# Two gated attention layers: ScalarE's order of key copies, exponential and token normalisation, and where the scores wait

## The chip, the cores and the metric

The kernel runs on one NeuronCore of a Trainium2 chip. Its engines work side by side and are ordered by semaphores alone: TensorE (PE, matmuls), VectorE (DVE), ScalarE (ACT), GpSimd (POOL) and SyncE (SP, which issues DMAs). The metric is the device time of one execution in microseconds. The kernel before took 2021.08 us, the median of 3 runs.

## The reference, cut to what matters

```python
x = x + tanh(g_xattn[0]) * L0_xattn(layernorm(x), ctx_768, ...)   # 8 heads of 64
x = x + tanh(g_ffn[0])   * L0_ffn(layernorm(x), ...)              # 16 experts, chosen by a Sinkhorn
x = x + tanh(g_xattn[1]) * L1_xattn(layernorm(x), ctx_768, ...)   # 16 heads of 64
x = x + tanh(g_ffn[1])   * L1_ffn(layernorm(x), ...)              # 2 of 8 experts for each sequence

# an attention:
q, k, v = x @ Wq, context @ Wk, context @ Wv
out = softmax(q @ k.T * 64 ** -0.5) @ v
out = out @ Wo + bo
```

x is 128 sequences of 64 tokens with 128 features, the context 128 x 64 x 96, all float32.

## The kernel before, in words

Tokens are worked on in 64 tiles of 128 (two sequences). `attention` builds both attention layers. The products of weights are folded beforehand: `AT` takes the context to keys that are multiplied directly with the tokens, `Bw` takes it to values that already hold the output projection. A step j handles one unit, a tile with 8 heads: the first attention has 64 units (G = 1), the second 128 (G = 2, two units for each tile; a unit "opens" its tile when it is the first of the two). Float16 operands are split in a high and a low part, which makes three products of each.

Each engine runs its own `body(j)` for every step, and in one body it handles several units at once: a is unit j, a1 is unit j-1, and so on. A semaphore wait at one point of an engine's order holds everything behind it. What belongs to step j, in the order in which each engine takes it:

- PE: in the second attention the transpose of the tile's normalised tokens (`psX`, L626, after ACT's `ln`), then the b half of the values of unit j-3 (L599), the keys of unit j in two halves of four heads, 24 matmuls each (L610, `psU`), the output product of unit j-4 (L654, `psY`, which waits for the transposed probabilities `PT` and for both value halves), the a half of the values of unit j-2 (L599), and the scores of unit j (L679, `psS`), two matmul pairs for heads 0 to 3, then two for heads 4 to 7. Ahead of the scores it waits for the tokens (`xt`), for both key copies (`uc0`, `uc1`) and for DVE's subtraction of the step before (`sub`). In the first attention the token transpose stands after the b values and is for the next unit, and a transpose of the context (L666) stands before the scores.
- ACT: normalised tokens (L713), high part of the values (L697, half a), transposed tokens `xTa` (L706), high part (L697, half b), the exponential of unit j-1 (L722, after `sub`), the two copies of the keys from PSUM (L728, 128 x 512 each, after `U0` and `U1` of PE), and the high part of the probabilities of unit j-2 (L733, after POOL's `mul`).
- DVE: low part of the values, half b (L802), sum of the exponentials of unit j-1 (L811) and its reciprocal (L813), residual (L817), maximum of the scores of unit j (L821), subtraction (L824), statistics for the next layer norm (L177), low part of the values, half a (L802). In the first attention it also works the layer norm of later tiles into some of its steps.
- POOL: bo added to x (L762, after `ln`), multiplication by the reciprocal (L776, unit j-1), low part of the probabilities (L781, unit j-2).
- SP: loads of context and keys, and the DMA transpose `PT<-Ph` of unit j-2 (L549).

In the second attention the keys of 40 tiles' second units (AHEAD = 40) were made earlier and lie in HBM. So in steps 0 to 79 the odd steps load their keys (L563, `a.loaded`) and only the even ones compute them; in steps 80 to 127 every step computes them. `phases` runs these two stretches, each with some steps in straight line and the rest in a hardware loop over 8 steps. There is one `psS`, and one `psU` bank for each half of the heads.

Of the kernel before, what the change touches and what calls it, by code (L numbers as in the profile page):

```python
# [18 lines left out]
ACT = mybir.ActivationFunctionType  # L19
# [10 lines left out]
AHEAD = 40  # L30
# [45 lines left out]
def wait(eng, sem, step, per=1, add=0):  # L76

    if isinstance(sem, Counter):
        sem, add = sem.handle, add + sem.start
    if step.reg is None and step.times(per, per + add) <= 0:  # L80
        return
    eng.wait_ge(sem, step.times(per, per + add))


def pipeline(eng, body, first, last, lo, hi, unroll):

    a = min(-(-lo // unroll) * unroll, last)
    n = max(0, (hi - a) // unroll)
    b = a + n * unroll
    for j in range(first, a):  # L90
        body(Step(None, 0, j))
    if n:
        with eng.Fori(0, n) as i:
            for u in range(unroll):
                body(Step(i, unroll, a + u))
    for j in range(b, last):
        body(Step(None, 0, j))
# [7 lines left out]
def _build(nc, whole, I, out):  # L105
# [66 lines left out]
    def column_of(t, tensor):  # L172
        return tensor[:, bass.ds(t.value, 1)]
# [166 lines left out]
    def attention(tag, G, Wq, Wk, Wv, Wo, bo, gate, ew=None, rw=None):  # L340

        first = ew is not None
        U = NT * G
        INNER = 512 * G
        s = Sems(tag)
        with ExitStack() as c:
# [154 lines left out]

                return (t - slot).div(n)

            def phases(eng, body, last, lo, hi):

                if first:
                    pipeline(eng, body, 0, last, lo, hi, 4)
                else:
                    pipeline(eng, body, 0, 2 * AHEAD, lo, 2 * AHEAD, RING * G)
                    pipeline(eng, body, 2 * AHEAD, last, 2 * AHEAD + 4, hi, RING * G)  # L510

            with nc.Block() as block:
# [76 lines left out]
                def _(e):  # L589
                    def body(j):  # L590
# [77 lines left out]
                        if a.on:  # L668
                            if a.opens:
                                wait(e, s["xt"], a.t)  # L670
                            if a.loaded:
                                wait(e, s[f"ul{a.tp}"], ring_of(a.t, 2, a.tp), 16)
                            else:
                                wait(e, s["uc0"], a.key())
                                wait(e, s["uc1"], a.key())
                            wait(e, s["sub"], a.j - 1)
                            for h in (0, 4):
                                for b in range(2):
                                    last = e.matmul(psS[half(b), h:h + 4, :], xT[:, a.tp, half(b)],  # L679
                                                    u[:, a.slot, h:h + 4, half(b)], start=True, stop=True)  # L680
                            last.then_inc(s["S"], 1)
# [7 lines left out]
                @block.scalar  # L689
                def _(e):  # L690
                    def body(j):
                        a, a1, a2, a3 = (Unit(j, k) for k in range(4))

                        def value_hi(a, b, name):
                            wait(e, s["V" + name], a.j)
                            wait(e, s["PV"], a.j - 2)
                            e.activation(vB[:, a.par, 0, b].rearrange("p k d -> p (k d)"), a.values(b),  # L697
                                         ACT.Copy).then_inc(s["vh" + name], 1)

                        nx = Unit(j, -1) if first else a  # L700

                        def tokens():
                            if nx.opens:
                                wait(e, s["X"], nx.t)
                                wait(e, s["S"], nx.j - G - 1)
                                e.activation(xT[:, nx.tp, :], psX, ACT.Copy).then_inc(s["xt"], 1)  # L706

                        if first and nx.on:
                            wait(e, s["C"], nx.t - 2)
                            e.activation(cc[:, nx.tp, 0, 0:DC], tile_of(nx.t, ctx32), ACT.Copy).then_inc(s["chi"], 1)  # L710
                        if nx.opens:
                            wait(e, s["X"], nx.t - 2)
                            e.activation(xn[:, nx.tp, :], tile_of(nx.t, x), ACT.Identity, bias=column_of(nx.t, nmr),  # L713
                                         scale=column_of(nx.t, rstd)).then_inc(s["ln"], 1)
                        if a3.on:
                            value_hi(a3, 0, "a")
                        tokens()
                        if a3.on:
                            value_hi(a3, 1, "b")
                        if a1.on:  # L720
                            wait(e, s["sub"], a1.j)
                            e.activation(E[:, a1.four], E[:, a1.four], ACT.Exp, bias=zero_col[:], scale=DH ** -0.5)\  # L722
                             .then_inc(s["exp"], 1)
                        if a.on and not a.loaded:
                            wait(e, s["S"], a.j - 2)
                            for b in range(2):
                                wait(e, s[f"U{b}"], a.key())
                                e.activation(u[:, a.slot, 4 * b:4 * b + 4].rearrange("p h l -> p (h l)"),  # L728
                                             psU[:, b, :], ACT.Copy).then_inc(s[f"uc{b}"], 1)
                        if a2.on:  # L730
                            wait(e, s["mul"], a2.j)
                            wait(e, s[f"pt{a2.par}"], ring_of(a2.j, 2, a2.par) - 1, 16)
                            e.activation(Ph[:, a2.par, 0].rearrange("p k t -> p (k t)"),  # L733
                                         E[:, a2.four].rearrange("p h l -> p (h l)"), ACT.Copy)\
                             .then_inc(s["phi"], 1)
                        if first and nx.on:
                            wait(e, s["C"], nx.t)
                            wait(e, s["Vb"], nx.j - RING)
                            wait(e, s[f"stored{nx.ring}"], ring(nx.t, nx.ring) - 1, 16)
                            e.activation(cT[:, nx.ring], psC[0:DC], ACT.Copy).then_inc(s["ct"], 1)  # L740
                    if first:
                        parts = (0, 8, 16, 32, 48, U)
                        for part, (lo, hi) in enumerate(zip(parts, parts[1:])):
                            e.wait_ge(s["nmr"], part + 1)
                            e.wait_ge(s[f"c{lo}"], 64 if lo >= 32 else 16)
                            pipeline(e, body, lo - 1, hi - 1 + 4 * (hi == U), max(lo - 1, 8), hi - 1, 4)
                    else:
                        e.wait_ge(s["nmr"], 1)
                        phases(e, body, U + 3, 8, U)

                @block.gpsimd
                def _(e):
# [1314 lines left out]
```

## Time and profile before

| | |
|---|---|
| median of 3 runs (2019.65 to 2022.82) | 2021.08 us |
| the profiled execution, its own time | 2019.13 us |
| its span, first to last instruction | 2017.3 us |
| mean granted TensorE clock | 0.969 of full |
| PE, DVE, ACT, POOL busy, share of the span | 92%, 80%, 77%, 32% |
| first attention | about 26 to 330 us |
| second attention | about 1322 to 1885 us |

Between the two lies the first feed-forward layer, behind them the second. How to read it: busy shares are averages over stages with different limits, and a busy PE is not a PE at its peak, since matmuls overlap in the records. For a group of matmuls the distance from its first start to the next group's first start is what counts.

### The profile page before, as it was taken

Reading aid. Unit: us, or ns where it says so; the run is one execution under the profiler, and the core shown is the slowest. Engines: PE = TensorE matmul, PEld = TensorE weight load, DVE = VectorE, ACT = ScalarE, POOL = GpSimd, SP = SyncE. Lnnn points to the kernel's source line nnn. Section 1 sums busy time; section 2 is a strip of 40 time slices with the busy share of each in tenths; the row PEclk is TensorE's granted clock in tenths of the full one; section 3 lists DMA queues with packets and bytes.
Section 4 is the critical chain, followed back from the end, with each engine's and each line's share of the span. In section 5 each row is a group of like instructions: output and inputs, shape, how many; then the busy total and the mean of one; then the engine's idle time right before and its main releaser. Section 6 shows DMA issues by size and latency. Waiting matters only on the chain. (4 is left out here: it accounts for less than half of the span.)

```text
span 2017.3 us, 73776 instructions
## 1 busy us (share of the span) xinstructions
PE 1851.8 (92%) x29130; PEld 1337.9 (66%) x29130; DVE 1610.9 (80%) x3619; ACT 1560.9 (77%) x2771; POOL 646.6 (32%) x893
## 2 busy tenths in 40 slices
PE   6999998884999999999999999868999999999698
PEld 5788886541666666666666667645666667777477
DVE  5989987796888888888888887767888887888544
ACT  4898896564998989899999898756777778787443
POOL 3787786210000000000000000034555555555465
PEclk9999998895999999999999999979999999999799
DMA  6645445391000000000000000045555554333233
GB/s 159 136 93 99 89 95 113 115 350 30 14 12 14 12 14 12 14 12 14 12 14 12 14 7 2 2 123 132 131 135 136 136 121 71 64 62 63 54 115 115
DMA packets 308079, 147.45 MB, mean 73 GB/s; under 512 B 235904, under 2 KB 294064, under 8 KB 307504
## 3 DMA queue, kind: packets, MB, share of 16 engines
q1 hardware_dynamic: 307328, 144.75, 29.2%
q8 instruction: 128, 2.10, 0.4%
q14 instruction: 63, 0.52, 0.1%
q10 hardware_dynamic: 560, 0.08, 0.0%
HBM read 55.45 MB, written 30.54 MB: 43 GB/s over the span
## 5 line engine op out<-in xcount | busy, mean ns | idle before, releaser
L1656 DVE TENSOR_TENSOR h<-g,h 128x1024 f16<-128x1024 f32 x256 | 313.2, 1223 | 140.7 <-ACT h L1601 140.6
L230 PEld LDWEIGHTS psE<-ew,h 128*128 128x128 f16 x6144 | 349.9, 98 | 54.5 <-issue 35.5
L230 PE MATMUL psE<-ew,h 128*128 128x128 f16 x6144 | 363.8, 219 | 11.8 <-DVE eo L1666 5.2
L230 PE MATMUL psH<-xg,ew 128*128 128x512 f16 x1536 | 355.6, 381 | 0.0
L1596 ACT ACTIVATE g<-psH,eb1T 128x512 f32<-128x512 f32 x512 | 330.3, 680 | 29.5 <-PE psH L230 23.0
L599 PE MATMUL psV<-Bw,cT 96*64 96x512 f16 x2304 | 319.5, 380 | 4.3 <-DVE vB L802 4.3
L776 POOL TENSOR_TENSOR E<-E,rden 128x512 f32<-128x512 f32 x192 | 200.0, 1042 | 325.9 <-DVE rden L813 325.9
L697 ACT ACTIVATE vB<-psV 128x512 f16<-128x512 f32 x384 | 226.7, 590 | 92.4 <-PE psV L599 92.3
L1601 ACT ACTIVATE h<-g 128x1024 f16<-128x1024 f32 x256 | 270.6, 1057 | 8.1
L1724 POOL MEMSET rbias<- 64x384 f32 x1 | 0.4, 411 | 854.8 <-POOLq L133 854.8
L230 PEld LDWEIGHTS psH<-xg,ew 128*128 128x128 f16 x1536 | 140.2, 98 | 183.9 <-issue 32.1
L802 DVE TENSOR_TENSOR vB<-psV,vB 128x512 f16<-128x512 f32 x384 | 248.0, 677 | 1.4 <-ACT vB L697 1.4
L610 PEld LDWEIGHTS psU<-cT,AT 96*64 96x64 f16 x7296 | 227.6, 111 | 16.7
L610 PE MATMUL psU<-cT,AT 96*64 96x128 f16 x7296 | 235.0, 221 | 0.0
L679 PE MATMUL psS<-u,xTa 128*64 128x256 f32 x1536 | 209.7, 393 | 20.4 <-ACT u L728 15.3
L821 DVE TENSOR_REDUCE top<-psS 128x8 f32<-128x512 f32 x192 | 132.1, 688 | 114.4 <-PE psS L679 114.2
L781 POOL TENSOR_TENSOR Ph<-E,Ph 128x512 f16<-128x512 f32 x192 | 222.0, 1157 | 3.7 <-ACT Ph L733 3.7
L654 PE MATMUL psY<-vB,PT 128*64 128x128 f16 x4608 | 167.2, 222 | 15.2 <-DMA PT<-Ph 14.4
L599 PEld LDWEIGHTS psV<-Bw,cT 96*64 96x64 f16 x2304 | 131.6, 110 | 62.0 <-DVE vB L802 7.9
L654 PEld LDWEIGHTS psY<-vB,PT 128*64 128x64 f16 x4608 | 144.1, 111 | 35.2 <-DMA PT<-Ph 33.9
L679 PEld LDWEIGHTS psS<-u,xTa 128*64 128x64 f32 x1536 | 105.0, 137 | 93.9 <-issue 64.5
L722 ACT ACTIVATE E<-E,zero_col 128x512 f32<-128x512 f32 x192 | 138.7, 722 | 35.2 <-DVE E L824 35.1
(256 smaller groups left out, 2813.9 us busy)
## 6 DMA issues: line engine op xcount, KB each, us to landing
keys_ahead<-ust SPq DMA_DIRECT2D x40, 512.0 KB, 4.9
u<-keys_ahead SPq DMA_DIRECT2D x40, 512.0 KB, 3.7
rawe<-in_L_ffn_w_dram SPq DMA_DIRECT2D x32, 256.0 KB, 3.2
wb<-rw SPq DMA_DIRECT2D x64, 128.0 KB, 2.0
rows<-places SPq DMA_DIRECT2D x110, 64.0 KB, 2.6
out_dram<-x SPq DMA_DIRECT2D x7, 512.0 KB, 3.2
context_T<-cT SPq DMA_DIRECT2D x64, 48.0 KB, 2.3
PT<-Ph SPq DMA_TRANSPOSE x192, 3.1
```

Of the source, the lines that this page charges most:

```text
L230: last = e.matmul(to, a, b, start=start and n == 0, stop=stop and n == 2, **flags)
L599: last = e.matmul(a.values(b)[half(hp)], cT[:, a.ring, cl, half(b)], Bw[:, bl, a.g, hp].rearrange("p k d -> p (k d)"), start=n == 0, stop= ...
L610: last = e.matmul(psU[half(m), b, to], AT[:, al, a.g, h, half(m)], cT[:, a.ring, cl, :], start=n == 0, stop=n == 2)
L654: last = e.matmul(psY[half(b), 0:D], PT[:, a4.par, pl, pair, half(b)], vB[:, a4.par, vl, b, pair, :], start=a4.g == n == pair == 0, stop=a ...
L679: last = e.matmul(psS[half(b), h:h + 4, :], xT[:, a.tp, half(b)], u[:, a.slot, h:h + 4, half(b)], start=True, stop=True)
L697: e.activation(vB[:, a.par, 0, b].rearrange("p k d -> p (k d)"), a.values(b), ACT.Copy).then_inc(s["vh" + name], 1)
L776: e.tensor_tensor(E[:, a1.four], E[:, a1.four], rden[:, a1.par, :].unsqueeze(2).broadcast_to([P, 8, N]), ALU.mult)\
L781: e.tensor_tensor(Ph[:, a2.par, 1].rearrange("p k t -> p (k t)"), E[:, a2.four].rearrange("p h l -> p (h l)"), Ph[:, a2.par, 0].rearrange( ...
L802: e.tensor_tensor(vB[:, a.par, 1, b].rearrange("p k d -> p (k d)"), a.values(b), vB[:, a.par, 0, b].rearrange("p k d -> p (k d)"), ALU.sub ...
L1596: e.activation(g32[:, ft, :], psH[:, ft, :], ACT.Gelu_apprx_tanh, bias=b1T[:, a.expert(1) * FT + ft:a.expert(1) * FT + ft + 1]).then_inc(s ...
L1601: e.activation(h[:, 1 - par, 0, ft - 1:ft + 1, :], g32[:, ft - 1:ft + 1, :], ACT.Copy).then_inc(s["h_hi"], 1)
L1656: e.tensor_tensor(h[:, 1 - par, 1, 2 * q:2 * q + 2, :], g32[:, 2 * q:2 * q + 2, :], h[:, 1 - par, 0, 2 * q:2 * q + 2, :], ALU.subtract)\
```

## The change

ACT's body gets two small functions, `normalised` (the tokens' layer norm) and `key_copy(b)` (one half of the keys). In both attentions the copy of heads 0 to 3 now stands ahead of the exponential, that of heads 4 to 7 behind it. PE's scores wait for `uc0` ahead of heads 0 to 3 and for `uc1` ahead of heads 4 to 7, and the wait for `sub` comes before both. In the second attention the normalised tokens of the next tile are made one step earlier, behind the second key copy and ahead of the high part of the probabilities; ACT therefore starts that attention with a step -1, and its last loop ends one step short, which leaves eight more of its steps in straight line. In the first attention the normalised tokens stay where they were.

```diff
@@ -501,12 +501,12 @@
 
                 return (t - slot).div(n)
 
-            def phases(eng, body, last, lo, hi):
+            def phases(eng, body, last, lo, hi, first_step=0):
 
                 if first:
                     pipeline(eng, body, 0, last, lo, hi, 4)
                 else:
-                    pipeline(eng, body, 0, 2 * AHEAD, lo, 2 * AHEAD, RING * G)
+                    pipeline(eng, body, first_step, 2 * AHEAD, lo, 2 * AHEAD, RING * G)
                     pipeline(eng, body, 2 * AHEAD, last, 2 * AHEAD + 4, hi, RING * G)
 
             with nc.Block() as block:
@@ -670,11 +670,10 @@
                                 wait(e, s["xt"], a.t)
                             if a.loaded:
                                 wait(e, s[f"ul{a.tp}"], ring_of(a.t, 2, a.tp), 16)
-                            else:
-                                wait(e, s["uc0"], a.key())
-                                wait(e, s["uc1"], a.key())
                             wait(e, s["sub"], a.j - 1)
                             for h in (0, 4):
+                                if not a.loaded:
+                                    wait(e, s[f"uc{h // 4}"], a.key())
                                 for b in range(2):
                                     last = e.matmul(psS[half(b), h:h + 4, :], xT[:, a.tp, half(b)],
                                                     u[:, a.slot, h:h + 4, half(b)], start=True, stop=True)
@@ -708,25 +707,35 @@
                         if first and nx.on:
                             wait(e, s["C"], nx.t - 2)
                             e.activation(cc[:, nx.tp, 0, 0:DC], tile_of(nx.t, ctx32), ACT.Copy).then_inc(s["chi"], 1)
-                        if nx.opens:
+                        def normalised(nx):
                             wait(e, s["X"], nx.t - 2)
                             e.activation(xn[:, nx.tp, :], tile_of(nx.t, x), ACT.Identity, bias=column_of(nx.t, nmr),
                                          scale=column_of(nx.t, rstd)).then_inc(s["ln"], 1)
+
+                        def key_copy(b):
+                            wait(e, s["S"], a.j - 2)
+                            wait(e, s[f"U{b}"], a.key())
+                            e.activation(u[:, a.slot, 4 * b:4 * b + 4].rearrange("p h l -> p (h l)"),
+                                         psU[:, b, :], ACT.Copy).then_inc(s[f"uc{b}"], 1)
+
+                        if nx.opens and first:
+                            normalised(nx)
                         if a3.on:
                             value_hi(a3, 0, "a")
                         tokens()
                         if a3.on:
                             value_hi(a3, 1, "b")
+                        if a.on and not a.loaded:
+                            key_copy(0)
                         if a1.on:
                             wait(e, s["sub"], a1.j)
                             e.activation(E[:, a1.four], E[:, a1.four], ACT.Exp, bias=zero_col[:], scale=DH ** -0.5)\
                              .then_inc(s["exp"], 1)
                         if a.on and not a.loaded:
-                            wait(e, s["S"], a.j - 2)
-                            for b in range(2):
-                                wait(e, s[f"U{b}"], a.key())
-                                e.activation(u[:, a.slot, 4 * b:4 * b + 4].rearrange("p h l -> p (h l)"),
-                                             psU[:, b, :], ACT.Copy).then_inc(s[f"uc{b}"], 1)
+                            key_copy(1)
+                        ahead = Unit(j, -1)
+                        if ahead.opens and not first:
+                            normalised(ahead)
                         if a2.on:
                             wait(e, s["mul"], a2.j)
                             wait(e, s[f"pt{a2.par}"], ring_of(a2.j, 2, a2.par) - 1, 16)
@@ -746,7 +755,7 @@
                             pipeline(e, body, lo - 1, hi - 1 + 4 * (hi == U), max(lo - 1, 8), hi - 1, 4)
                     else:
                         e.wait_ge(s["nmr"], 1)
-                        phases(e, body, U + 3, 8, U)
+                        phases(e, body, U + 3, 8, U - 1, -1)
 
                 @block.gpsimd
                 def _(e):
```

## Rows read from the trace of the kernel before

**Rows 1.** The page of the profile: busy time, share and instructions of each engine
```profile
PE 1851.8 (92%) x29130; PEld 1337.9 (66%) x29130; DVE 1610.9 (80%) x3619; ACT 1560.9 (77%) x2771; POOL 646.6 (32%) x893
```

**Rows 2.** Windows: stretch, its length, then busy us (instructions) of PE, PEld, DVE, ACT, POOL
```profile
1386.00:1661.00 275.00, 261.49 (x4668) 173.98 (x4664) 240.41 (x469) 209.69 (x401) 157.11 (x166) 1.00 0.55 133
1662.00:1880.00 218.00, 214.43 (x4530) 162.19 (x4524) 176.31 (x340) 174.81 (x338) 114.63 (x122) 1.00 0.36 64
```

**Rows 3.** Timeline, full stretch: start, duration, engine, line, operation, [idle before <-releaser]
```profile
1754.36 1.08 PE L679 MATMUL psS<-u,xTa 128*64 128x256 f32 x8
...
1755.27 0.82 PE L599 MATMUL psV<-Bw,cT 96*64 96x512 f16 x6
...
1755.92 1.51 PE L610 MATMUL psU<-cT,AT 96*64 96x128 f16 x48
...
1756.94 0.72 ACT L722 ACTIVATE E<-E,zero_col 128x512 f32<-128x512 f32 x1 [0.21 <-DVE E L824]
...
1757.26 0.85 PE L654 MATMUL psY<-vB,PT 128*64 128x128 f16 x24
1757.57 1.06 ACT L728 ACTIVATE u<-psU 128x512 f32<-128x512 f32 x2
...
1757.93 0.82 PE L599 MATMUL psV<-Bw,cT 96*64 96x512 f16 x6
1758.02 0.68 DVE L811 TENSOR_REDUCE den<-E 128x8 f32<-128x512 f32 x1
...
1758.87 1.08 PE L679 MATMUL psS<-u,xTa 128*64 128x256 f32 x8
```

**Rows 4.** Timeline, one pair of steps in the mixed stretch
```profile
1450.43 1.08 PE L679 MATMUL psS<-u,xTa 128*64 128x256 f32 x8 [0.20 <-ACT u L728]
...
1451.56 0.69 DVE L821 TENSOR_REDUCE top<-psS 128x8 f32<-128x512 f32 x1 [0.88 <-PE psS L679]
...
1453.51 1.03 PE L679 MATMUL psS<-u,xTa 128*64 128x256 f32 x8
...
1454.22 0.58 SPq L563 DMA_DIRECT2D u<-keys_ahead  x1
...
1454.69 0.44 PE L626 MATMUL psXC<-ident,xna 128*64 128x128 f32 x4 [0.15 <-ACT xna L713]
...
1454.96 0.82 PE L599 MATMUL psV<-Bw,cT 96*64 96x512 f16 x6
...
1456.08 1.16 POOL L781 TENSOR_TENSOR Ph<-E,Ph 128x512 f16<-128x512 f32 x1
...
1456.71 0.72 ACT L722 ACTIVATE E<-E,zero_col 128x512 f32<-128x512 f32 x1 [0.30 <-DVE E L824]
...
1457.27 1.24 SPq L549 DMA_TRANSPOSE PT<-Ph  x1
...
1457.62 0.82 PE L599 MATMUL psV<-Bw,cT 96*64 96x512 f16 x6
...
1458.64 1.08 PE L679 MATMUL psS<-u,xTa 128*64 128x256 f32 x8 [0.20 <-ACT u L728]
...
1460.36 0.81 PE L654 MATMUL psY<-vB,PT 128*64 128x128 f16 x22
```

**Rows 5.** DMA transfers in 1400 to 1660: keys (KB, median us), and landings of PT
```profile
u<-keys_ahead SPq DMA_DIRECT2D x31, 512.0 KB, 3.7
...
DMA to landing us min/median/max: 3.0/3.1/3.1
```

**Rows 6.** Timeline, first attention, one step
```profile
197.75 0.72 ACT L722 ACTIVATE E<-E,zero_col 128x512 f32<-128x512 f32 x1
...
199.08 0.67 DVE L811 TENSOR_REDUCE den<-E 128x8 f32<-128x512 f32 x1
...
200.82 0.69 DVE L821 TENSOR_REDUCE top<-psS 128x8 f32<-128x512 f32 x1 [0.39 <-PE psS L679]
```

**Rows 7.** Score matmuls, L679, first attention: idle us and times, by releaser
```profile
  ACT u L728: 7.1, 14
```

## The prediction

> **What bounds the kernel now.** I read the page first, for where TensorE (PE) is dense, then the table of windows over the two long stretches of the second attention, then the timeline of one pair of steps in each stretch, and last the same for the first attention. PE is the busiest engine of the page [rows 1]. The second attention has 128 steps, two for each tile of tokens. In the first 80, which I call the mixed stretch, only every other step computes keys (the other loads them); in the last 48, the full stretch, every step does. In the table the mixed stretch has PE busy 261.5 of 275 us and VectorE (DVE) 240.4, the full stretch 214.4 and 176.3 of 218 [rows 2]. Busy does not say back to back, because a matmul's modelled end overlaps the next one's start, so I go by starts. In the full stretch the groups without a wait take: scores (L679) 0.91 us (1754.36 to 1755.27), the b values (L599) 0.65 (to 1755.92), the keys (L610) 1.34 (to 1757.26) and the output product (L654) 0.67 (to 1757.93), together 2.01. The a values need the same 0.65, so the next scores could start at 1758.58. They start at 1758.87, a gap of 0.29 [rows 3]. What came last before them is ScalarE (ACT): both copies of the keys end at 1757.57 + 1.06 = 1758.63, and 0.24 us later the scores start. Those copies stand behind the exponential, which waited for DVE's subtraction and started at 1756.94 [rows 3]. In the mixed stretch the same wait is larger: a values at 1457.62, scores possible at 1458.27, started 1458.64, so 0.37; the idle note on the row names ACT's copy [rows 4]. There are two more gaps in that pair: the token transpose (psXC, L626) starts 1454.69, though the scores before it, started at 1453.51, need only 0.91, so 0.27 (the row names ACT's normalised tokens), and the output product starts at 1460.36, 1.72 us after scores that with the b values need 1.56, so 0.16 [rows 4]. That product waits for the DMA transpose of the probabilities.
>
> **The change part by part.** Per step nothing is added or removed on an engine; ACT's order changes, two PE waits move, and the normalisation of a tile's tokens (second attention only) runs one step earlier.
>
> *Low keys ahead of the exponential, full stretch.* The low four heads are the first 24 of the 48 matmuls that start at 1755.92: they end by some 0.65 + 0.22 later, about 1756.8, so the copy runs 1756.8 to 1757.4 (1.06 us for the two overlapping copies, so 0.48 to 0.59 each). The exponential starts at about 1757.3 instead of 1756.94, ends at about 1758.0, and the high copy ends at about 1758.5, against 1758.63 [rows 3]. The low scores need the low copy alone and can start at 1758.58; the high ones come 0.45 later, at 1759.03, and need 1758.5 + 0.24 = 1758.74. So the 0.29 goes. In the tile's other step the same sum of PE starts leaves 0.06; it goes too. That is 0.35 us for each of 24 pairs: 8.4 us. What could be late next is the sum of exponentials on DVE (L811), which starts at 1758.02 [rows 3]: the exponential now ends at almost that instant, a shift under 0.1 us, and behind that sum DVE waits for the scores anyway.
>
> *The same, mixed stretch.* The loaded step has no key copy to move. In the step with keys the 0.37 goes by the same sum: the exponential moves from 1456.71 [rows 4] to about 1457.0, the high copy ends some 0.2 earlier than now, and the low scores start at 1458.27.
>
> *Tokens one step earlier.* The normalisation takes 0.49 us of ACT, and now stands in the odd step between the exponential and the copy of the probabilities; it ends near 1454.1 and covers the 0.27 before the transpose [rows 4]. Queued behind it is that copy (L733), 0.4 us later, for which POOL has no use before 1456.08, where its subtraction starts [rows 4]. In the full stretch PE has no gap there, so nothing is gained or lost. Extra straight-line code at ACT's end (eight steps leave its last loop) I cost at nothing: ACT is busy 174.8 of the 218 us [rows 2].
>
> *What is late next in the mixed stretch.* Without the gaps PE needs, for a pair, 0.91 + 0.27 + 0.65 + 2.01 + 0.65 for the step with keys and 0.91 + 0.65 + 0.67 + 0.65 for the loaded one: 7.37. DVE runs without a pause except the 0.88 before the maximum (L821): 8.21 - 0.88 = 7.33 [rows 4]. But a longer ring goes through the DMA. From the maximum at 1451.56, DVE's work without pause, POOL's low part of the probabilities (ends 1456.08 + 1.16), the transpose issued at 1457.27 and landing 3.1 later, to the output product at 1460.36 are 8.80 us. From there PE needs 0.67 + 0.65 + 0.91 + 0.27 + 0.65 + 2.01 + 0.65 = 5.81 to the scores of the next step with keys, and 1.13 pass from scores to maximum (1450.43 to 1451.56) [rows 4]. The ring is 15.74 us and closes after two pairs: 7.87 for a pair. So of the 0.80 of gaps only 8.21 - 7.87 = 0.34 comes out, and the wait for the transposed probabilities grows from 0.16 to about 0.5. A window of 275 us holds 33 such pairs [rows 2], 11.2 us; the first five pairs of the attention, before and in a stall that this change does not touch, I give half, 0.85. If the ring did not hold, it would be up to 0.80 x 33 = 26; if it were longer, nothing.
>
> Here a rule bears. The row of the 512 KB keys load shows it issued at 1454.22 and the list of transfers gives it 3.7 us, so it is on its way until about 1457.9, while the transpose from 1457.27 lands after 3.1, as all of this stretch do [rows 4, 5]: an overlap of 0.65 us at no visible cost. In the new order the two get closer by 0.34, since the load follows the odd step's transpose, which moves with the earlier pair. The Trainium skill ("DMA: Bandwidth & Descriptors", section "Issuing engines are not separate DMA queues") says that DMAs all run on the same 16 engines and interleave. By it the transpose could land up to 0.34 later; the trace so far does not bear that out.
>
> *First attention.* The exponential at 197.75 would wait for the low keys' copy and move to about 198.26, end at 198.98 instead of 198.47, and the sum (L811) starts at 199.08: it just fits. Both copies together end when they did, since ACT does the same work in another order. If the exponential came later than that, DVE has another 0.39 before its maximum at 200.82 [rows 6]. The score matmuls of this attention waited for key copies in 14 places only, 7.1 us together [rows 7]; those are steps in which DVE was behind with the layer norm and set the pace. I take 0, with bounds from a loss of 2 to a gain of 7.
>
> **The sum.** 8.4 + 11.2 + 0.85 + 0 = 20.4 us. The profiled execution took 2019.13 (span 2017.3): it would be 1998.7. The median of the three runs is 2021.08, 1.95 above it, and I put the forecast against that: 2000.7.
>
> **Rivals.**
> (a) The DMA ring is worse: the transpose lands later by the nearness to the keys load, 0.34 or more. The ring is then 16.08 or more, 8.04 a pair, and the mixed stretch gives 0.17 x 33 = 5.6 instead of 11.2. With the five early pairs giving nothing and the full stretch 6 to 8.4, the time is 2007 to 2010. For it: the ring has no slack. Against: no transpose of the stretch took over 3.1 us [rows 5].
> (b) The ring gives way, because the transpose or POOL is quicker than I chained them, and PE's 7.37 or a DVE near it binds: the mixed stretch gives 0.6 to 0.8 a pair, 20 to 26 us, the time is 1985 to 1992.
> (c) Slower: the exponential now stands behind a wait for PE's low keys. If ACT sees those 0.5 us later than I read from the starts, the exponential ends 0.5 later, the sum with it, and through DVE the maximum, the subtraction and the next exponential. It decides from the point where the exponential ends more than 0.39 us after the sum's old start, for then DVE's pause is eaten up. The price is then 0.1 to 0.2 a step over 64 + 128 steps, 19 to 38 us, while the gains of PE's waits vanish: 2035 to 2060. Against it: the starts put that end 0.1 before the old start in the first attention.
> (d) No effect: the copies' place was not what held the scores, but something that ended with them, such as the wait for the previous subtraction; 2017 to 2025. Against it: that subtraction had ended before the exponential started, 1.9 us ahead of the scores [rows 3].
>
> **How the numbers follow.** Forecast with its own spread (1996 to 2006) 0.60, (a) 0.14, (b) 0.10, (c) 0.08, (d) 0.08. The range goes from 1990, which takes in the nearer part of (b), to 2011 with all of (a). About 0.2% (4 us) is what a measurement can tell from no change. Forecast, (a) and (b) are faster: 0.84; (d) is within: 0.08; (c) is slower: 0.08.
>
> **What would show it.** Right: in the full stretch maxima every 4.33 us instead of 4.50; scores starting 0.65 after the a values in all steps; in the mixed stretch pairs of 7.87 and a wait of about 0.5 us for the transposed probabilities before the output product, with none for normalised tokens; the first attention as long as before. Wrong: mixed pairs near 7.4 (b) or 8.05 (a); a transpose landing later than 3.1; a DVE wait before the sum of exponentials in most steps (c); scores that still start 0.24 after a copy of the keys (d).

## The result, and the profile after

The changed kernel took 1987.26 us, the median of 4 runs (1986.04 to 1990.99); the kernel before, on the same chip, 2021.36. The ratio is 0.9835, 95% interval 0.9818 to 0.9852. That is 34 us faster. The forecast was 2000.7 with a range from 1990 to 2011: the direction was right, and the time lies below the range, where rival (b) had been put (1985 to 1992), but not by the mechanism of (b). The row that follows gives each engine's busy time in us, its share of the span and its number of instructions.

The profiled execution of the changed kernel took 1987.86 us (span 1986.1), 31.3 less than that of the kernel before. The page's row of busy times hardly differs from [rows 1]:

```profile
PE 1830.3 (92%) x29130; PEld 1319.6 (66%) x29130; DVE 1617.8 (81%) x3619; ACT 1563.8 (79%) x2771; POOL 647.9 (33%) x893
```

The windows of the two long stretches, in the columns of [rows 2] (the mixed stretch lies a little earlier now):

```profile
1386.00:1641.00 255.00, 239.85 (x4524) 171.46 (x4522) 234.96 (x454) 203.29 (x390) 153.77 (x162) 1.00 0.59 139
1642.00:1847.00 205.00, 205.00 (x4508) 161.03 (x4504) 176.61 (x336) 172.97 (x334) 113.42 (x121) 1.00 0.39 68
```

In the full stretch the records show PE busy for all of the 205 us, where [rows 2] had 214.4 of 218. The timeline of one step there, in the columns of [rows 3]:

```profile
1754.44 0.60 ACT L718 ACTIVATE u<-psU 128x512 f32<-128x512 f32 x1
...
1754.93 0.71 ACT L732 ACTIVATE E<-E,zero_col 128x512 f32<-128x512 f32 x1
...
1755.55 0.59 ACT L718 ACTIVATE u<-psU 128x512 f32<-128x512 f32 x1
1755.57 0.82 PE L599 MATMUL psV<-Bw,cT 96*64 96x512 f16 x6
1755.68 0.69 DVE L820 TENSOR_REDUCE den<-E 128x8 f32<-128x512 f32 x1
...
1756.22 1.03 PE L678 MATMUL psS<-u,xTa 128*64 128x256 f32 x8
...
1757.09 0.82 PE L599 MATMUL psV<-Bw,cT 96*64 96x512 f16 x6
```

The order on ACT is as forecast: low copy at 1754.44, exponential at 1754.93, high copy at 1755.55, and the sum of exponentials (now L820) at 1755.68 was not held up. The scores start at 1756.22, 0.65 after the a values at 1755.57: the gap of 0.29 of [rows 3] is gone. What I had not forecast is the next distance: from the scores to the b values it is 0.87 (1756.22 to 1757.09), where [rows 3] has 0.91.

The mixed stretch, in the columns of [rows 4]:

```profile
1550.65 1.03 PE L678 MATMUL psS<-u,xTa 128*64 128x256 f32 x8
...
1551.51 0.81 PE L599 MATMUL psV<-Bw,cT 96*64 96x512 f16 x6
...
1552.29 0.86 PE L654 MATMUL psY<-vB,PT 128*64 128x128 f16 x24
...
1553.64 1.03 PE L678 MATMUL psS<-u,xTa 128*64 128x256 f32 x8
...
1554.50 0.39 PE L626 MATMUL psXC<-ident,xna 128*64 128x128 f32 x4
...
1557.38 0.81 PE L599 MATMUL psV<-Bw,cT 96*64 96x512 f16 x6
...
1557.53 1.23 SPq L549 DMA_TRANSPOSE PT<-Ph  x1
...
1558.03 1.03 PE L678 MATMUL psS<-u,xTa 128*64 128x256 f32 x8
...
1560.63 0.86 PE L654 MATMUL psY<-vB,PT 128*64 128x128 f16 x24 [0.92 <-DMA PT<-Ph]
...
1566.37 0.81 PE L678 MATMUL psS<-u,xTa 128*64 128x256 f32 x6
```

The last row counts 6 matmuls and not 8, because the view ended at 1567. The token transpose (L626) starts 0.86 after the scores at 1553.64, without the 0.27 of [rows 4]. The wait for the transposed probabilities has grown from about 0.17 a pair to 0.60 on average over the stretch, and here it comes unevenly: the output product at 1552.29 is 0.78 after the b values at 1551.51 and so nearly free, the one at 1560.63 stood idle for 0.92. Scores with keys start at 1550.65, 1558.03 and 1566.37: one pair of 7.38, one of 8.34, together 15.72. That fits the ring of the prediction, 15.74, which "closes after two pairs".

How long a pair takes on average can be read from the maxima of the scores (one for each step). Here are the 69 maxima from the 13th step of the second attention on, 34 pairs, of the kernel before and then of the changed one; the columns are durations in ns, then first and last start:

```profile
L821 DVE TENSOR_REDUCE top<-psS x69: 677/690/692, 1385.6 to 1665.7; 128x8 f32<-128x512 f32 x69
```

```profile
L830 DVE TENSOR_REDUCE top<-psS x69: 678/691/693, 1378.9 to 1645.8; 128x8 f32<-128x512 f32 x69
```

280.1 / 34 = 8.24 us a pair before, 267.0 / 34 = 7.85 after. (The full stretch is given below by the same maxima, over the 47 steps behind them, so 23.5 pairs.) In the first attention the score matmuls also changed, which can be seen next to the group before them. The kernel before, one step (context transpose, scores, b values):

```profile
199.54 0.29 PE L666 MATMUL psXC<-ident,cc 128*64 128x128 f16 x4
...
199.70 1.08 PE L679 MATMUL psS<-u,xTa 128*64 128x256 f32 x8
...
200.58 0.85 PE L599 MATMUL psV<-Bw,cT 96*64 96x512 f16 x6
```

The changed kernel (high copy of the keys, sum of exponentials, context transpose, scores, b values):

```profile
199.27 0.59 ACT L718 ACTIVATE u<-psU 128x512 f32<-128x512 f32 x1
...
199.48 0.68 DVE L820 TENSOR_REDUCE den<-E 128x8 f32<-128x512 f32 x1
...
199.88 0.29 PE L666 MATMUL psXC<-ident,cc 128*64 128x128 f16 x4
...
199.99 1.04 PE L678 MATMUL psS<-u,xTa 128*64 128x256 f32 x8
...
200.86 0.82 PE L599 MATMUL psV<-Bw,cT 96*64 96x512 f16 x6
```

From context transpose to scores it was 0.16 and is 0.11, and from scores to b values 0.88 and 0.87. The high copy starts at 199.27 and ends, after its 0.59, at 199.86; with the 0.24 that a copy's end is ahead of the scores it would have let them start at 200.10, but the low ones started at 199.99. An ordinary step, from one maximum of the scores to the next, takes 4.51 us instead of 4.59.

That is the smaller part of what the first attention gained. The larger came mostly in the steps that follow those of 5.0 to 5.6 us, in which DVE works the layer norm in. The kernel before, two maxima behind such a stretch and the scores between them:

```profile
97.28 0.68 DVE L821 TENSOR_REDUCE top<-psS 128x8 f32<-128x512 f32 x1
...
100.67 1.08 PE L679 MATMUL psS<-u,xTa 128*64 128x256 f32 x8 [0.39 <-ACT u L728]
...
101.79 0.69 DVE L821 TENSOR_REDUCE top<-psS 128x8 f32<-128x512 f32 x1 [0.46 <-PE psS L679]
```

The same two maxima in the changed kernel:

```profile
95.21 0.68 DVE L830 TENSOR_REDUCE top<-psS 128x8 f32<-128x512 f32 x1
...
99.19 0.68 DVE L830 TENSOR_REDUCE top<-psS 128x8 f32<-128x512 f32 x1
```

Before, the scores waited 0.39 for ACT's copies, DVE then waited 0.46 for the scores, and the step took 4.51. Now neither waits and it takes 3.98.

By stretch, the two profiled executions: first attention 299.7 to 294.2 us, first twelve steps of the second 57.0 to 55.8, mixed stretch 280.1 to 267.0, full stretch 211.6 to 201.3, and what is left, which the change does not touch, 1168.9 to 1167.8.

### The profile page after: what moved, and what is told of

It is laid out like the page before. It is cut to its first block and busy times, and to the rows that moved or that the text cites. A ratio compares the mean times of both kernels' runs of the same rounds, so it can differ in the third digit from the quotient of the medians.

```text
span 1986.1 us, 73780 instructions
## 1 busy us (share of the span) xinstructions
PE 1830.3 (92%) x29130; PEld 1319.6 (66%) x29130; DVE 1617.8 (81%) x3619; ACT 1563.8 (79%) x2771; POOL 647.9 (33%) x893
## 5 line engine op out<-in xcount | busy, mean ns | idle before, releaser
L678 PE MATMUL psS<-u,xTa 128*64 128x256 f32 x1536 | 201.0, 382 | 2.5 <-DVE E L833 1.9
L718 ACT ACTIVATE u<-psU 128x512 f32<-128x512 f32 x304 | 179.9, 592 | 14.9 <-PE psU L610 5.3
L599 PEld LDWEIGHTS psV<-Bw,cT 96*64 96x64 f16 x2304 | 120.3, 111 | 79.6 <-DVE vB L811 14.6
L732 ACT ACTIVATE E<-E,zero_col 128x512 f32<-128x512 f32 x192 | 137.4, 716 | 11.3 <-DVE E L833 10.7
```

Source lines behind the costliest of these rows:

```text
L599: last = e.matmul(a.values(b)[half(hp)], cT[:, a.ring, cl, half(b)], Bw[:, bl, a.g, hp].rearrange("p k d -> p (k d)"), start=n == 0, stop= ...
```

## The experiments

All were timed in three rounds beside the kernel before (2020.4 to 2021.7 us, 7 to 19 runs in each comparison). The first four take the change apart.

**Only the split of PE's wait.**

```diff
-                                wait(e, s["uc0"], a.key())
-                                wait(e, s["uc1"], a.key())
                             wait(e, s["sub"], a.j - 1)
                             for h in (0, 4):
+                                if not a.loaded:
+                                    wait(e, s[f"uc{h // 4}"], a.key())
```

> The kernel before with one edit on TensorE: the scores of heads 0 to 3 wait for the first key copy, those of heads 4 to 7 for the second. ScalarE's order is that of before. Theory A (the split of the wait carries the gain): in the kernel before the first of the two copies ends some 0.5 us before the second, by 1758.15 in the rows of the full stretch, 0.24 us later is 1758.39, and the scores could start at 1758.58 without any wait; the second half comes 0.43 later than the first, after 1758.87. So the wait goes without any move on ScalarE. Full stretch 8.57 us a pair as in the changed kernel, first attention 4.51 us a step, mixed stretch 7.8 to 7.95 a pair although the token transpose still waits for the normalised tokens, because the ring through the DMA transpose is longer than that. Time 1986 to 1992. Theory B (the first copy has to stand ahead of the exponential): scores keep waiting in every step with keys, time above 2010.

1993.05 us, ratio 0.9864 (0.9848 to 0.9881): 28 of the 34 us, with ACT's order untouched. The timeline in the full stretch, with ACT's copies merged in one row as they follow each other (L727):

```profile
1751.86 1.06 ACT L727 ACTIVATE u<-psU 128x512 f32<-128x512 f32 x2
...
1752.14 0.82 PE L599 MATMUL psV<-Bw,cT 96*64 96x512 f16 x6
...
1752.79 1.04 PE L678 MATMUL psS<-u,xTa 128*64 128x256 f32 x8
...
1753.88 0.44 PE L626 MATMUL psXC<-ident,xna 128*64 128x128 f32 x4
```

The second copy ends at 1751.86 + 1.06 = 1752.92; the scores started at 1752.79, before that, and 0.65 after the a values. So the first copy alone had let them go. The maxima of the mixed stretch:

```profile
L820 DVE TENSOR_REDUCE top<-psS x69: 678/690/692, 1377.1 to 1644.2; 128x8 f32<-128x512 f32 x69
```

267.1 / 34 = 7.86 us a pair, as in the changed kernel. An ordinary step of the first attention takes 4.51 us, and the whole of it is 5.1 us shorter than before. Theory A holds, with a time 1 us above its range. It was off in the full stretch, which takes 8.78 us a pair and not 8.57: the rows show why, since the token transpose at 1753.88 comes 1.09 after the scores instead of 0.86. It waits for ACT's normalised tokens, 0.14 to 0.23 in each pair, a wait that the score gap had covered in the kernel before. In the mixed stretch hardly anything of it is left, 0.07 in every fourth pair, because the ring is the longer one there. With the scores released by the split alone, the wait for the transposed probabilities comes evenly, 0.50 to 0.60 in nearly every pair, and the pairs take 7.79 to 7.88.

**Only ACT's order of copies** (low copy ahead of the exponential, PE waits for both before any score, tokens in their old place).

```diff
+                        if a.on and not a.loaded:
+                            key_copy(0)
                         if a1.on:
                             wait(e, s["sub"], a1.j)
...
                         if a.on and not a.loaded:
-                            wait(e, s["S"], a.j - 2)
-                            for b in range(2):
...
+                            key_copy(1)
```

> The kernel before with ScalarE's first key copy ahead of the exponential and nothing else: the scores wait for both copies ahead of heads 0 to 3, tokens are normalised where they were. Theory A: the second copy ends only 0.13 us earlier in one step of a full pair and 0.09 later in the other, so of 0.35 us of gaps 0.3 stays: full stretch 8.9 to 9.0 us a pair. Mixed stretch: 0.2 of the 0.37 comes out, 8.0 to 8.1. First attention as before or 0.03 a step slower. Time 2011 to 2018. Theory B (the order carries the gain): time below 2000. In both, scores that start after a wait still take 0.89 to 0.91 us to the next group, not 0.86.

2015.65 us, ratio 0.9976 (0.9966 to 0.9986). The score instructions in the full stretch between 1662 and 1840, and for how long their engines sat idle ahead of them (matmuls and weight loads together):

```profile
L679 PE MATMUL psS<-u,xTa x320: 379/379/430, 1663.0 to 1838.2; 128*64 128x256 f32 x160
...
  issue: 17.9, 40
```

All 40 steps there still have their gap. The 17.9 us do not measure it: they are idle time of the weight loads, one place in each step. By starts the scores come 0.15 later than the 0.65 after the a values, 6.1 us over the 40 steps, where the kernel before has 6.9 over 39. From the scores to the next group it is 0.91 in 32 of the 40, and 0.88 to 0.93 in the others. A mixed pair takes 8.10, a full one 8.95, both as expected; an ordinary step of the first attention 4.67 instead of 4.59, since the second copy now ends later and all scores wait for it. So the part of the change that I had costed as its core is worth 6 us by itself.

**Only the tokens one step earlier.**

```diff
-                        if nx.opens:
+                        if nx.opens and first:
...
                             key_copy(1)
+                        ahead = Unit(j, -1)
+                        if ahead.opens and not first:
+                            normalised(ahead)
...
-                        phases(e, body, U + 3, 8, U)
+                        phases(e, body, U + 3, 8, U - 1, -1)
```

> The kernel before with the tokens of the next tile normalised one step earlier and nothing else. Theory A (the mixed stretch is then still held by the ring scores, maximum, subtraction, exponential, both copies, scores, 8.21 us a pair, which does not go through the token transpose): the 0.27 us before the transpose goes and comes back in full as a longer wait before the next scores; time within 2 us of before. Theory B (TensorE's gaps add up): 0.27 to 0.31 us for each of 34 to 40 pairs, 9 to 12 us faster.

2020.81 us, ratio 0.9998 (0.9988 to 1.0008). Mixed pairs stay at 8.24 and full ones at 9.01: the wait before the token transpose is gone and came back before the next scores, which now start about 1.4 after the a values where it was 1.0.

**The change without the tokens.** Against the changed kernel:

```diff
-                        if nx.opens and first:
+                        if nx.opens:
                             normalised(nx)
...
-                        ahead = Unit(j, -1)
-                        if ahead.opens and not first:
-                            normalised(ahead)
...
-                        phases(e, body, U + 3, 8, U - 1, -1)
+                        phases(e, body, U + 3, 8, U)
```

> The changed kernel with the tokens normalised in their old place. Theory A: the mixed stretch is held by the ring through the DMA transpose, so the token transpose waits again for ScalarE but the output product waits the less: 7.85 to 7.95 us a pair, time within 4 us of the changed kernel. Theory B (gaps add up): 0.27 for each of 34 to 40 pairs comes back, 9 to 12 us slower than the changed kernel.

1988.47 us, ratio 0.9841 (0.9824 to 0.9857), 1.2 from the changed kernel, less than its runs differ. Mixed pairs 7.86. In the full stretch a pair takes 8.64 instead of 8.57, so there the tokens' move is worth 0.07 a pair, 1.7 us by the two profiles.

The next ones ask what holds the mixed stretch at 7.85.

**The low part of the probabilities first.** In the second attention GpSimd subtracts for unit j-2 ahead of its multiplication for unit j-1.

```diff
+                        def mul():
                             if a1.on:
                                 wait(e, s["rden"], a1.j)
...
+                        def low():
                             if a2.on:
                                 wait(e, s["phi"], a2.j)
...
+                        for part in ((low, mul) if not first else (mul, low)):
+                            part()
```

> The changed kernel; in the second attention GpSimd makes the low part of the probabilities of unit j-2 ahead of the multiplication of unit j-1, not behind it. It then no longer waits for VectorE's reciprocal of the same step, so the transpose is issued some 1.4 us earlier in the steps that close the ring. Theory R (the mixed stretch is held by the ring through the DMA transpose, 7.85 us a pair in three kernels so far): the stretch falls to what TensorE's groups add up to, 7.28, or to VectorE's 7.33: 7.3 to 7.5 us a pair, the wait of the output product for the transpose is gone, and the kernel takes 1970 to 1976. Full stretch and first attention as in the changed kernel. Rival (the 7.85 comes from something else, such as the exponential or VectorE's order): 7.8 to 7.9 a pair, 1985 to 1990.

1965.38 us, ratio 0.973 (0.9713 to 0.9746): 22 us faster than the changed kernel, and 5 below the range expected. Rows of the timeline: ACT's high part, POOL's low part, DVE's reciprocal, POOL's multiplication, the transpose, and the next output product but one:

```profile
1551.17 0.61 ACT L742 ACTIVATE Ph<-E 128x512 f16<-128x512 f32 x1
...
1551.86 1.16 POOL L793 TENSOR_TENSOR Ph<-E,Ph 128x512 f16<-128x512 f32 x1 [1.31 <-ACT Ph L742]
1551.94 0.20 DVE L828 RECIPROCAL rden<-den 128x8 f32<-128x8 f32 x1
...
1552.97 1.04 POOL L786 TENSOR_TENSOR E<-E,rden 128x512 f32<-128x512 f32 x1
1553.04 1.24 SPq L549 DMA_TRANSPOSE PT<-Ph  x1
...
1556.41 0.84 PE L654 MATMUL psY<-vB,PT 128*64 128x128 f16 x24
```

The low part at 1551.86 no longer waits for the reciprocal, which starts at 1551.94; in the changed kernel it started after it (1556.34 and 1555.05). The maxima of the mixed stretch:

```profile
L836 DVE TENSOR_REDUCE top<-psS x69: 675/681/693, 1372.0 to 1621.8; 128x8 f32<-128x512 f32 x69
```

249.8 / 34 = 7.35 us a pair, what PE and DVE were said to need by themselves (7.37 and 7.33). The output product now starts 0.65 after the b values in all but three pairs. Between the two profiled executions, 24.7 us apart, the mixed stretch makes 17.2, the first twelve steps 3.3 and stages that nothing here touches 4.1. So the edit itself is worth about 20 us, and the kernel comes out below the expected range partly by luck. It is faster than both kernels of the comparison.

**Keys loaded twice.** The second load goes to a buffer that nobody reads, and the scores wait for both.

```diff
+                        e.dma_start(twin[:, a.tp].rearrange("p h l -> p (h l)"),
+                                    keys_ahead[bass.ds(a.t.value, 1)].rearrange("o p k -> p (o k)"))\
+                         .then_inc(s[f"ul{a.tp}"], 16)
```

> The changed kernel; each load of keys from HBM is followed by a second one of the same 512 KB into a buffer that nobody reads, and the scores wait for both. Theory C (the DMAs share engines, so a transpose behind a load lands later, and the ring turns that into time): landings of the transposes go from 3.1 to 3.5 us or more in the mixed stretch, and a pair takes longer by half of what is added on the ring, 8.05 or more; 1994 or more. Rival (the loads leave the transposes alone): 3.1 us, 7.85 a pair, time of the changed kernel within 2 us.

1998.85 us, ratio 0.9904 (0.9875 to 0.9932), 11.6 more than the changed kernel. Two transfers of the list (KB and us to landing), the second load, issued at 1555.95, and the transpose issued behind it at 1558.13:

```profile
twin<-keys_ahead SPq DMA_DIRECT2D x1, 512.0 KB, 4.5
```

```profile
PT<-Ph SPq DMA_TRANSPOSE x1, 3.4
```

In the mixed stretch the transposes behind the doubled load land after 3.2 to 4.6 us, 3.55 on average, the others after 3.0 to 3.1, one of them after 3.3. The maxima:

```profile
L835 DVE TENSOR_REDUCE top<-psS x69: 679/691/693, 1382.9 to 1656.9; 128x8 f32<-128x512 f32 x69
```

274.0 / 34 = 8.06 a pair, 0.21 more, about half of the 0.49 by which every other transpose is late on average. The other 6 us came in the first twelve steps (62.0 us instead of 55.8), around a stall that I did not look into. So the rule that the engines are shared (the Trainium skill, "DMA: Bandwidth & Descriptors", section "Issuing engines are not separate DMA queues") does bear here, but only from a larger overlap on. In the changed kernel the single load (1554.62, 3.6 us) is on its way for 0.7 us beside the transpose of 1557.53, and that one lands after 3.1 as before; here it is 2.3 us. The changed kernel itself has three transposes in this stretch that the load overlaps by more than 1.5 us. They landed after 3.16, 3.53 and 3.55; the one issued at 1596.16:

```profile
PT<-Ph SPq DMA_TRANSPOSE x1, 3.5
```

Its other 29 overlapped transposes, by 0.66 to 1.41 us, took 3.05 to 3.08.

**A longer ring, first try.** One more 128x128 addition on GpSimd between the multiplication and the low part, in the even steps.

```diff
+                        if not first and a.ahead and a.on and a.par == 0:
+                            e.tensor_tensor(spare[:, a.four], bo_rep[:], bo_rep[:], ALU.add)
```

> The changed kernel; in the even steps of the mixed stretch GpSimd does one more addition of 128x128 (0.45 us) between the multiplication and the low part of the probabilities, with nothing else touched. Theory R: the ring of two pairs is 0.45 us longer, a pair 0.22: 8.07 to 8.09 us, 7.5 to 9 us more in all than the changed kernel. Rival (GpSimd is not on what holds the stretch): no change, since GpSimd is busy under 60% of it. A rival within the theory (the ring closes after one pair): 0.45 a pair, 15 to 18 us more.

1988.78 us, ratio 0.984 (0.9824 to 0.9856): as the changed kernel. The addition, the low part, its transpose, an output product, and the transpose of the odd step:

```profile
1551.96 0.40 POOL L791 TENSOR_TENSOR spare<-bo_rep 128x128 f32<-128x128 f32 x1
...
1552.32 1.16 POOL L794 TENSOR_TENSOR Ph<-E,Ph 128x512 f16<-128x512 f32 x1
...
1553.50 1.23 SPq L551 DMA_TRANSPOSE PT<-Ph  x1
...
1556.75 0.84 PE L656 MATMUL psY<-vB,PT 128*64 128x128 f16 x24
...
1557.29 1.23 SPq L551 DMA_TRANSPOSE PT<-Ph  x1
```

The maxima, 268.2 / 34 = 7.89 a pair:

```profile
L834 DVE TENSOR_REDUCE top<-psS x69: 678/691/693, 1377.6 to 1645.8; 128x8 f32<-128x512 f32 x69
```

This was an error of the experiment: the addition stood in the wrong steps. The even step's transpose, issued at 1553.50, lands 3.1 later at 1556.6, and its output product starts at 1556.75: it has slack, and less of it than before. The ring goes through the odd step's (1557.29), where nothing was added.

**A longer ring, in the odd steps.**

```diff
-                        if not first and a.ahead and a.on and a.par == 0:
+                        if not first and a.ahead and a.on and a.par == 1:
```

> As e8_ring_longer, but the extra addition on GpSimd (0.40 us there) stands in the odd steps of the mixed stretch. The trace of the changed kernel shows that the transposes for which the output product waits (issued at 1549.19 and 1557.53) are those of the odd steps; in e8 the addition stood in the even ones, whose transposes have slack. Theory R (ring of two pairs through the odd step's transpose): 0.36 to 0.40 us on the ring, 0.18 to 0.20 a pair, 8.03 to 8.05 us, 6 to 8 us more than the changed kernel in all. Rival (GpSimd's order is not on what holds the stretch): 7.85 as before. Rival (ring closes in one pair): 8.2 to 8.25.

1993.41 us, ratio 0.9867 (0.985 to 0.9883), 6 more than the changed kernel. The maxima:

```profile
L834 DVE TENSOR_REDUCE top<-psS x69: 672/691/692, 1377.3 to 1650.0; 128x8 f32<-128x512 f32 x69
```

272.7 / 34 = 8.02 a pair, 0.17 more for 0.36 to 0.40 on the ring. In the even steps the same addition gave 0.04. This is what a ring that closes after two pairs and goes through the odd step's transpose would give; one that closes after a single pair would have given 0.36 to 0.40.

**The kernel before with the low part first.** The edit of e5_low_part_first, on the kernel before.

> The kernel before with the low part of the probabilities ahead of the multiplication on GpSimd in the second attention, and nothing of the change. Theory R: in the kernel before another ring binds (scores, maximum, subtraction, exponential, both copies, scores: 8.21 us a pair), so the same edit that gained 22 us on the changed kernel gains next to nothing here: within 3 us of before, 8.15 to 8.25 a pair in the mixed stretch. Rival (the edit is worth its time in any kernel): 15 us or more faster.

2020.87 us, ratio 0.9999 (0.9989 to 1.0008), 8.24 a pair. The wait for the transposed probabilities is gone (the output product starts 0.65 after the b values, where it was about 0.82), and the pair is as long as it was. What was worth about 20 us on the changed kernel is worth nothing on the kernel before, where the ring through the scores and ACT's copies is the longer one.

## Why the prediction was wrong in size, point by point

*Full stretch: 8.4 forecast, 10.3 measured.* The gaps of 0.35 a pair went, as said. The mis-sized term is PE's own: I took 0.91 as what the scores need, from scores that had themselves waited. Those that do not wait need 0.864 to 0.866: in every kernel with the split, and also in the loaded steps of e3_tokens_ahead_only, which has no split. Where they wait, as in e2_copy_order_only, it is mostly 0.909. That is 0.045 a step, 0.09 a pair, 2.2 us. I had called the groups of [rows 3] "without a wait", and that one was not.

*Which part does it: wrong.* I gave the 8.4 to the low copy ahead of the exponential and did not ask what the split alone would do. [Rows 3] had the answer: the two copies start at 1757.57 and take 1.06 together, so the low one ends near 1758.15, and 0.24 later is before 1758.58. The split alone brought 28 us, the order of copies alone 6, the tokens alone nothing. The order adds about 5 us once the scores are split, mainly in the full stretch, 8.78 to 8.64 a pair. My claim that tokens one step earlier gain nothing there was wrong too: their wait appears when the score gap goes (0.14 to 0.23 a pair in e1_split_wait_only), which the forecast looked for in the mixed stretch only.

*Mixed stretch: 11.2 forecast, 13.1 measured.* The mechanism held: 7.87 forecast, 7.85 measured, in three kernels that differ on ACT, and longer or shorter when the ring was made so. The difference is on the side of before, where I multiplied a pair of 8.21 while the average is 8.24, and in 34 pairs for 33. The wait for the transposed probabilities grew to 0.60 on average, unevenly in the changed kernel and evenly (0.55) in the two others, where 0.5 was forecast. The first twelve steps gave 1.2 for the 0.85 forecast. Rival (a), the transpose delayed by the keys load, happened to 3 of the 65 transposes and not to the rest; it happens to every other one when the load is doubled.

*First attention: 0 forecast, 5.6 measured.* This is the step that failed, and the one that took the time out of the range: with the 5.6 us put back it would have been 1992.9. I had the right view, 7.1 us of waits for key copies in 14 places [rows 7], and put it at nothing with the words that DVE "was behind with the layer norm and set the pace" there. It set the pace in the layer norm's own steps. In those behind them it had caught up and waited for the scores, which waited for both copies: 4.51 us where 3.98 was possible. Of the 14 waits for the copies, one of 0.35 is left. These steps, the first five and the last gave 3.2 us net. The other 2.4 are 30 ordinary steps of 0.08 each, which that view does not list, since it has only idle time between the modelled end of one matmul and the start of the next. The starts show them: scores 0.16 to 0.18 after the context transpose where 0.11 is enough, and 0.88 instead of 0.87 to the next group. I had gone by starts in the second attention and not here. One step near the start takes 0.9 longer in some executions than in others, in either kernel, so single profiles are uncertain by that much; the seven kernels with the split gained 5.1 to 6.7 us here. The bound of +7 in the text covered it, the value taken did not. The sum of exponentials was not late, as forecast [rows 6].

*The sum.* 10.3 + 13.1 + 1.2 + 5.6 = 30.2 of the 31.3 us between the two profiled executions; 1 us is in stages that the change does not touch, and those took between 1163.7 and 1169.9 us in the eleven profiled executions. The medians are 34.1 apart, because the profiled execution of before was 2.2 below its median and that of the changed kernel 0.6 above. The measured time is 13.4 below the forecast: 5.6 from the first attention, 4.2 from the three terms of the second, which were all too small, 1 from the untouched stages, and the rest is the scatter of the executions. The range reached 10.7 below the forecast, enough for any one of these and not for all.

*The rivals.* (b) names the right time for a wrong reason: the ring did not give way, and mixed pairs near 7.35 came only with GpSimd's order changed. (c), the exponential held up behind the keys, did not show: the sum at 1755.68 follows the exponential (1754.93 + 0.71) at once, and DVE still waits for the scores in all 42 steps of the full stretch between 1662 and 1840. (d) fell with e1_split_wait_only.

## What to carry to other kernels

A consumer that waits for two producers and needs the first alone to begin should wait for each in its place; read when the first one ends before anything is moved on the producer's engine. What a group of matmuls needs is to be read where nothing was waited for, by its distance from start to start, and compared between stretches. When a wait is removed, add up the rings: the next longest gives the time of the stretch, it can close only after two rounds, and an edit that is worth nothing before (GpSimd's order) may be worth 20 us once that ring binds. And a list of idle times needs two more questions before a place in it is put at nothing: who waited behind it, and which waits are too short to be listed.

## What was not expected of the hardware

The eight score matmuls that the trace lists for a step take 0.864 us from their first start to the next group's when they follow the group before without a wait. When the first of them waited on a semaphore it is 0.909 in most steps, and 0.885 in the first attention and in some steps of the second. The traces do not show where the 0.02 to 0.045 goes. A wait in the middle of the group, with its semaphore already at its value, cost nothing that shows: the steps with that wait take 0.864, like the loaded steps that have none.

A DMA transpose of the probabilities lands after 3.0 to 3.1 us when a 512 KB load of keys, issued before it, is on its way for up to 1.4 us beside it, as when none is. This holds for all but one of the mixed stretch in the kernel before, with only the split, and changed; the exception, in the kernel before, took 3.57 at 0.7 us. With more than 1.5 us of overlap it takes longer: 3.16 to 3.55 in the changed kernel, 3.13 to 3.46 in e5_low_part_first (twelve, at 1.48 to 1.78 us), and 3.2 to 4.6 behind the doubled load (at 2.1 to 3.6 us). Why the first 1.4 us cost nothing, the traces do not show.
